# The skip term of a Mamba layer moved from a VectorE operation into a PSUM accumulation on TensorE

## The reference

```
x, z = split(xn @ in_proj_w.T);  x = silu(conv4(x))          # 256 channels each
s_t = s_{t-1} * exp(delta_t * A) + (delta_t * x_t) * B_t      # 16 states per channel
y_t = sum over the 16 states of s_t * C_t
y = y + x * Dskip
y = y * silu(z)
out = y @ out_proj_w.T
```

## Time and profile before

| | |
|---|---|
| median of 3 runs | 1236.87 us (1236.36 to 1238.31) |
| span of the profiled execution, first to last instruction | 1232.9 us |
| DVE busy | 1070.5 us (87%) |
| PE busy | 1022.4 us (83%) |
| POOL busy | 858.9 us (70%) |
| ACT busy | 734.7 us (60%) |
| mean granted TensorE clock | 0.901 |

### The profile page before, as it was taken

The page is one execution under the profiler, slowest core; times in us unless marked ns, Lnnn a source line. Parts: engine busy times, 40 slices in busy tenths (PEclk is TensorE's granted clock), DMA queues, the critical chain, the costliest instruction groups (busy, mean ns, idle before and its releaser), DMA issues.

```text
span 1232.9 us, 15308 instructions
## 1 busy us (share of the span) xinstructions
PE 1022.4 (83%) x3821; PEld 476.4 (39%) x3821; DVE 1070.5 (87%) x1331; ACT 734.7 (60%) x1117; POOL 858.9 (70%) x708
## 2 busy tenths in 40 slices
PE   0755858999999899999999997888888888888785
PEld 0522324444545454444445453333333333243322
DVE  7647968889898979899898989999898989999996
ACT  2564535767586776767685766556564756555421
POOL 2335788767676867677676769687777868686755
PEclk9988868999999999999999999788887979797765
DMA  6542325243432424342534423442434333343311
GB/s 160 157 94 68 91 79 130 57 99 69 107 80 64 103 62 111 77 94 51 119 68 98 89 57 80 86 86 48 87 71 90 81 73 68 82 85 80 72 36 34
DMA packets 81065, 103.01 MB, mean 84 GB/s; under 512 B 13280, under 2 KB 51072, under 8 KB 81024
## 3 DMA queue, kind: packets, MB, share of 16 engines
q1 hardware_dynamic: 76928, 94.18, 35.3%
q0 software_dynamic: 4096, 8.40, 2.3%
HBM read 18.66 MB, written 16.78 MB: 29 GB/s over the span
## 4 chain that ended last, share of the span: by engine, by line
PE 40%; DVE 24%; issue 22%; POOL 7%; ACT 3%; DVEq 1%; DMA 1%; SPq 1%; POOLq 0%; ACTq 0%
DVE u_sb L902 10%; DVE s_sb L972 8%; PE bank L1204 6%; PE bank L1171 5%; PE bank L1189 5%; PE bank L1127 4%; PE bank L1182 4%; PE bank L1114 3%; POOL expert_in L585 3%; PE bank L1135 2%; PE bank L1136 2%; PE bank L1137 2%; POOL s_sb L578 2%; PE bank L1147 2%; DVE g_sb L860 2%
## 5 line engine op out<-in xcount | busy, mean ns | idle before, releaser
L578 POOL TENSOR_TENSOR s_sb<-s_sb,c_of 128x512 f32<-128x512 f32 x480 | 628.5, 1315 | 273.2 <-DVE s_sb L972 265.1
L972 DVE TENSOR_TENSOR_SCAN s_sb<-bank,u_sb 128x512 f32<-128x512 f32 x512 | 620.4, 1212 | 0.0
L762 ACT ACTIVATE bank<-bank,a_neg 128x510 f32<-128x510 f32 x512 | 334.0, 659 | 255.9 <-PE bank L1189 246.4
L902 DVE TENSOR_TENSOR u_sb<-bank,b_of 128x512 f32<-128x512 f32 x512 | 346.2, 676 | 98.7 <-PE bank L1182 94.9
L1182 PE MATMUL bank<-dsp,sel_d 128*128 128x512 f32 x512 | 316.1, 617 | 39.8 <-DVE u_sb L902 20.4
L1189 PE MATMUL bank<-dsp,sel_d 128*128 128x512 f32 x512 | 244.5, 478 | 79.0 <-DVE s_sb L972 71.5
L1182 PEld LDWEIGHTS bank<-dsp,sel_d 128*128 128x128 f32 x512 | 104.6, 204 | 243.4 <-DVE u_sb L902 147.6
L1189 PEld LDWEIGHTS bank<-dsp,sel_d 128*128 128x128 f32 x512 | 106.5, 208 | 195.4 <-DVE s_sb L972 163.0
L1204 PE MATMUL bank<-s_sb,con 128*32 128x512 f32 x1024 | 161.2, 706 | 12.7 <-POOL s_sb L578 6.8
L1114 PE MATMUL bank<-xnT,wx 128*128 (+1 forms) x256 | 128.8, 597 | 0.0
L585 POOL DMA_INDIRECT expert_in<-xn,put_at x64 | 65.6, 1026 | 17.9 <-issue 17.8
(11 more groups left out here) (140 smaller groups left out, 1045.0 us busy)
## 6 DMA issues: line engine op xcount, KB each, us to landing
b_of<-bc SPq DMA_DIRECT2D x64, 256.0 KB
c_of<-bc SPq DMA_DIRECT2D x64, 256.0 KB
dsp<-hi SPq DMA_DIRECT2D x64, 256.0 KB
dsp<-dd SPq DMA_DIRECT2D x64, 256.0 KB
expert_in<-dd SPq DMA_DIRECT2D x8, 512.0 KB, 6.4
xn<-expert_in SPq DMA_DIRECT2D x8, 512.0 KB, 5.4
xn<-L_ffn_W SPq DMA_DIRECT2D x16, 256.0 KB, 4.6
expert_out<-xn SPq DMA_DIRECT2D x16, 256.0 KB, 2.4
```

The costliest lines, as they stand in the source:

```text
L578: pool.tensor_tensor(s_now, s_now, c_of[:, hf, hh, :], ALU.mult).then_inc(S["p_ready"], 1)
L762: act.activation(d, d, ACT.Exp, scale=a_neg[:, k:k + 1]).then_inc(S["decay_ready"], 1)
L902: dve.tensor_tensor(u_sb[:, w % U_RING, :], du_ps[w % 2][:, :], b_of[:, hf, head_of(w), :], ALU.mult).then_inc(S["u_ready"], 1)
L972: dve.tensor_tensor_scan(s_sb[:, w % S_RING, :], decay_of(w)[:, :], u_sb[:, w % U_RING, :], 0.0, ALU.mult, ALU.add).then_inc(S["scan_done" ...
```

## The change

A diagonal matrix skip_w with Dskip on its diagonal is made once for each half in the setup. In sum_quad, before the first sum of a half, PE multiplies x by it with start=True; the sums that follow all accumulate. `gate_half` is one product of the PSUM bank and silu(z). The semaphore y_read is gone: PE's first write to the bank in the next half waits for g_ready.

```diff
-GATE = (5, 6)
+GATE = 5
...
+        skip_w = sb("skip_w", [P, HALVES, P])
...
+            dve.wait_ge(S["w_loaded"], 16 * W_LOADS)
+            for hf in range(HALVES):
+                dve.tensor_scalar(skip_w[:, hf, :], ident, dsk[:, hf:hf + 1], None, ALU.mult
+                                  ).then_inc(S["skip_ready"], 1)
...
-            def gate_half(ch, hf, step):
-
-                if step == 0:
-                    dve.wait_ge(S["sum_done"], per_chunk(ch, SLOTS // QUADS, UNITS // QUADS * (hf + 1)))
-                    dve.scalar_tensor_tensor(g_sb[:, hf, :], xs_of(ch, hf), dsk[:, hf:hf + 1], y_ps[:, :],
-                                             ALU.mult, ALU.add).then_inc(S["y_read"], 1)
-                else:
-                    dve.wait_ge(S["y_read"], per_chunk(ch, 2, hf + 1))
-                    dve.tensor_tensor(g_sb[:, hf, :], g_sb[:, hf, :], zs_of(ch, hf), ALU.mult
-                                      ).then_inc(S["g_ready"], 1)
+            def gate_half(ch, hf):
+
+                dve.wait_ge(S["sum_done"], per_chunk(ch, SLOTS // QUADS, UNITS // QUADS * (hf + 1)))
+                dve.tensor_tensor(g_sb[:, hf, :], y_ps[:, :], zs_of(ch, hf), ALU.mult).then_inc(S["g_ready"], 1)
...
-                    wait(pe, "y_read", per_chunk(ch, 2, k * QUADS // UNITS))
+                    hf = k * QUADS // UNITS
+                    wait(pe, "g_ready", per_chunk(ch, 2, hf))
+                    pe.matmul(y_ps[:, :], skip_w[:, hf, :], xs_of(ch, hf), start=True, stop=False)
                 wait_products(pe, ch, QUADS * (k + 1))
                 for q in range(QUADS):
                     mm = pe.matmul(y_ps[q * 32:(q + 1) * 32, :], con[:, K_SUM + 32 * r:K_SUM + 32 * (r + 1)],
                                    s_sb[:, (QUADS * k + q) % S_RING, :],
-                                   start=(r == 0), stop=(r == UNITS // QUADS - 1))
+                                   start=False, stop=(r == UNITS // QUADS - 1))
...
+            pe.wait_ge(S["skip_ready"], HALVES)
```

More of the change, by code:

```diff
@@ L197, in bass_mamba_moe @@
             "scattered du_spread delta_spread u_ready decay_ready scan_done p_dve p_ready sum_done "
-            "y_read g_ready misc_pe misc_act misc_dve misc_bc b_loaded0 b_loaded1 c_loaded0 c_loaded1 sp_act sp_chain "
+            "skip_ready g_ready misc_pe misc_act misc_dve misc_bc b_loaded0 b_loaded1 c_loaded0 c_loaded1 sp_act sp_chain "
             "dx_ready dd_ready hi_ready lo_ready stacked ffn_loaded eo_free b1_ready take_ready back_loaded "
@@ L980, in body @@
                                           ).then_inc(S["p_dve"], 1)
[L982 to L986, removed]
+                    if w == GATE and ch[0] > 0:
+                        gate_half(before(ch), 1)
+                    if w == UNITS + GATE:
+                        gate_half(ch, 0)
                     if not low_by_pool(ch):
@@ L1015, in last @@
                 ins.then_inc(S["combine_last"], 1)
-                gate_half(end, 1, 0)
-                gate_half(end, 1, 1)
+                gate_half(end, 1)
                 dve.wait_ge(S["combine_last"], 1)
```

## The result

The changed kernel took 1245.36 us (median of 4 runs, 1245.09 to 1247.75), the kernel before 1236.76 in the same rounds (1236.36 to 1238.31). The ratio is 1.0074, with a 95% interval of 1.006 to 1.0089: slower by 8.6 us, where 4.9 us of gain were forecast, and outside the range given.

The account below looks back on a forecast made before the run. No engine bounds everywhere: DVE and PE alternate within a chunk. Gains of 1.1 (expert chunks), 0.6 (combine chunks) and 3.2 us (last chunk) sum to 4.9, giving 1232.0 us from 1236.9, range 1225.5 to 1239.0.

Parts of the forecast that it names:

- First gate: Expert chunk, first gate: L1200 delays spreads and B/C matmul, which starts 0.33 us late; less old slack, +0.2 us.
- old slack at L872: Expert chunk, end of the output projection: under 0.1 us to spare at L872 on DVE, taken off the 0.33 us delay.
- Second gate: Expert chunk, second gate: L1200 fills PE's pauses, second layer starts at 579.0 instead of 579.36, a gain of 0.35 us.
- rival 1: PE is the bound behind each gate: expert-chunk gates lose 0.35 us each, slow-clock gates 0.3, kernel 1241 us; chance 0.17.
- Combine chunks: Chunks 9 to 14: gain 0 at the first gate, 0.1 us a chunk taken overall, 0.6 us for six.
- quoted rule: VectorE with two SBUF inputs contends with GpSimd reading SBUF; the new gate frees POOL, but the sum stays the same.
- clock rival: L1200 fills PE's gaps in combine chunks, the clock rises, second gates gain 0.6 instead of 0.1: 1228 us; chance 0.13.
- 1.8 us for L1200 at half clock: Combine chunks, second gate: clock at 0.50, L1200 costs 1.8 us, u comes 0.2 to 0.3 late.
- gain of 0 around the first gate: Combine chunks, first gate: ACT is held by POOL's memset and DVE's next u waits for PE, so gain 0.
- DVE's saving: The one-product gate saves DVE 0.63 us a half, 20.2 us over 32 halves if DVE set the pace everywhere.
- Last chunk and tail: PE has room for L1200: first gate gains 1.4 us, second 1.0, tail's L860 0.8, together 3.2 us.

Follow-up runs that it names:

- e1: Changed kernel with the skip matmul on PE, but DVE keeping both gate steps (first with factor zero): 1242.6 us, ratio 1.0053 to the kernel before.
- e3: Changed kernel with skip matmuls moved in PE's order, half 0's behind the third sum (slot 14), half 1's behind slot 23's expert matmul: 1232.47 us, ratio 0.9977.
- e10: e6 with half 1's skip matmul ahead of slot 23's expert matmul instead of behind it: one run of 1239.38 us.
- e6: Changed kernel with half 0's skip matmul in slot 8, ahead of the B/C matmul, and half 1's in slot 23 behind the expert matmul: 1233.21 us, ratio 0.9996.
- e2: Changed kernel with the one-operation gate on DVE but no skip matmul, so x * Dskip is left out: 1236.76 us, ratio 1.0007.
- e7: e6 with the combine operations from slot 16 on: 1223.74 us, ratio 0.9922.
- e9: e6 with the combine operations of chunks 9 to 14 in slots 18 to 25: 1225.54 us, ratio 0.992.
- e11: e6 with both gate steps kept on DVE (first with factor zero): 1234.89 us, ratio 0.9998.
- e8: The kernel before with only the combine operations moved, from slot 16 on: 1242.12 us, ratio 1.007.
- e4: Changed kernel with the combine operations of chunks 9 to 14 in slots 16 to 23 instead of 14 to 21: 1229.28 us, ratio 0.9946.
- e5: e3 and e4 together, skip matmuls in slots 14 and 23 and combine operations from slot 16 on: 1225.05 us, ratio 0.9923.

## Why the prediction was wrong

Two steps failed in their reasoning: in the expert chunks the start of the second layer, put at 579.0 without its wait for ACT, and in the combine chunks the time of DVE's operations between the gates, taken as constant. A third had the right mechanism and a wrong size, the first gate of an expert chunk.

**First gate (forecast +0.2 us, measured +0.5).** The mechanism was the forecast one, the size was off. The working had the second spread at 2.92 behind the gate and the B/C matmul at 6.57; they stand at 3.10 and 6.74. L1200 with the change of weights took 1.05 from its start to the sum's, not 0.98, and it started 0.72 behind the gate, where the forecast had 0.71. The remaining 0.1 lies between the sum's start and the second spread (1.33 against 1.23). And of the old slack at L872, from which the forecast took its way down from 0.33 to 0.2, nothing was had: L871 is later by the whole 0.5. e1 (+0.55) and e3 (-0.06) show that it is L1200's place.

**Second gate (forecast -0.35, measured +0.23).** This step failed in its reasoning. "The second layer starts at 579.0" assumed that it follows the spreads of slot 24, which came at 4.60 behind the gate as worked out (4.58). It depends on ACT's relu of the expert matmul that L1200 pushed back. In the timeline of the kernel before, at the end of the stretch of the earlier trace rows:

```profile
577.04 1.02 PE L1164 MATMUL bank<-xn 128*128 128x512 f32 x2
...
578.21 0.68 ACT L737 ACTIVATE xn<-bank,b_now 128x512 f32<-128x512 f32 x1
...
579.36 1.95 PE L1171 MATMUL bank<-xn 128*128 128x128 f32 x16
```

The relu ends at 578.89, 1.85 us behind the expert matmul's start and inside the 0.63 us that PE waits for the scan up to 579.02, so no wait for ACT was to be seen. In the changed kernel the expert matmul stands 3.51 behind the gate, and with those 1.85 the relu can't be ready before 5.36 by this row; measured, L1168 starts at 5.31. The forecast spent a pause of PE without asking what else it covered. e10 against e6 shows the link, by 0.58 us. The two gates together cost 0.73 us a quiet expert chunk, about the 0.70 of rival 1, which had a chance of 0.17; but rival 1 put the second gate's loss on PE's time alone.

**Clock in expert chunks (not forecast).** In one of chunks 3 to 8 the clock fell, for 1.5 us. The change made the wait before the B/C matmul 1.91 us instead of 0.93; PE's part alone makes it 1.49 (e1) and DVE's part alone 1.53 (e2). In the kernel before a wait of 0.63 us for a scan stands shortly ahead of it, so PE's idle time grew by less than these numbers say. In the eight traces, those of before and of the change among them, in which this wait is 0.91 us or more, 12 of the 56 chunks 2 to 8 have a stretch at half clock, one to three in each trace. In e6, e7, e9 and e10, where it is 0.68 at most, and in e11, where PE doesn't wait there, none of 35 has one. So with the pause filled no such fall was seen.

But the length of the wait doesn't tell which chunk falls: 1.91 us gave one fall and 1.53 three, and e8, whose expert chunks are those of the kernel before, has one in chunk 8. The Trainium skill, TensorE: Matmul & The Clock Gate, section HAM oscillation, says that idle gaps bring the clock down; e6 agrees in this, as filling the gap left chunks 2 to 8 at 1.00, and the 44 chunks that kept full clock with the gap show that the gap alone doesn't decide.

**Combine chunks (forecast -0.1 each, measured +1.1 to +2.3 in chunks 10 to 14).** The forecast looked at the two gates only. From L872 in slot 11 to slot 18 DVE runs without a wait, and I took its operations there as constants. One of them is 1.6 us longer because of POOL's run.

Five chunks with 1.6 make 8.1 us, and the +8.05 measured equals it only because the other slots cancel over the five: some 13 us are gained, 6.0 of them in slots 6 and 22 and 6.8 in slot 27, and as much is lost, in slots 1, 7 to 11, 19, 23 and 31. Only the long operation is the same in each of the five; the step from +1.1 to +2.3 is that of slots 19 and 23. e1, whose slots 1, 27 and 31 show nearly the changed kernel's pattern, has none of the five long operations and stands at +0.35: beside it the changed kernel has lost 8.1 us more in slot 14, and what it lost more in slots 7 to 11, 19 and 23 (6.9) about returned what the gates gave (6.0).

The same operations moved by two slots change the span by -15.5 us in e4, and by +4.9 in e8, on the kernel before. e1 and e2 show that it is DVE's part of the change that brings the long operations, e11 that it isn't the saved operation by itself. What decides is one interval, from DVE's L872 to the start of POOL's run. The kernel before, the changed one and the six versions with the combine operations in slot 14 have 48 such chunks: in 37 the run begins 0.04 to 1.24 us behind L872, and each has a long operation, the longer the later the run; in 11 it begins 0.46 to 1.22 us ahead, and none has one. That a chunk without a long operation is shorter as a whole isn't shown: chunks 10 to 14 are at +1.99 in e3 with five that cost 11.3 us in slot 14, and at -2.31 in e7 with five, and e9 is no faster than e7.

The quoted rule of the Trainium skill (SBUF — State Buffer, Who interferes with whom) was drawn on for L864 and POOL, and dismissed as of no effect on the sum. The same rule names the pair that decided: a combine operation is a VectorE one with two SBUF inputs, and the traces agree with the rule there, 0.33 us with no product running and 1.96 beside POOL's run.

**The clock rival was half true.** The forecast's 1.8 us for L1200 at half clock was not met: in the chunk shown it took 1.06, slot 22 gained the whole 0.60 us, and slot 27 1.37 where the clock had been at half. The mean clock of the combine window rose from 0.85 to 0.92. The gain was spent in the same chunk: slot 1 lost 0.4 to 1.05 us, slots 7 and 8 to 11 0.3 and 0.45, slot 31 0.4, and in every other chunk slot 19 lost 1.1 and slot 23 0.7. The forecast's gain of 0 around the first gate was thus some 0.2 of loss.

**DVE's saving.** 20.2 us of DVE work in the quiet rows were worth 0.38 us an expert chunk with no L1200 at all (e2), 0.27 beside one well placed (e11 to e6). In such a chunk of e6 slots 6 and 22 are 0.60 us shorter each, and slots 9, 11 and 26, where DVE waits for PE, 0.30, 0.30 and 0.46 longer. That DVE waits for PE, on which the forecast was built, held.

**Last chunk and tail (forecast -3.2, measured -2.1).** The tail's gate went as forecast. The chunk lost 1.40 in slot 7 again, of 1.61 gained in slot 6, and the tail waited 2.82 us for gathered rows where it had waited 2.40, so part of DVE's gain only made that wait longer.

**Open.** Why the half-clock stretches of the combine chunks fall where they do, and with them the 0.4 to 1.1 us in slots 1 and 19, was seen and not tested. Nor is it settled why e3, e6 and e11, each with six long operations, stand in chunks 10 to 14 at +1.99, +6.16 and +4.35. The 11.6 us between the changed kernel and e4 in these chunks is four times what its long operations account for: five of some 1.9 us gave way to three of some 2.0.

## What to carry to other kernels

When work is moved to an in-order engine, follow every consumer behind it through the other engines, and ask of each pause that it fills what the pause was covering. When an engine gets faster, look for what it will now run beside: an operation of constant work isn't one of constant time, and a shift of half a microsecond against another engine's burst brought 1.6 us a chunk here, where the two removed operations had given 1.2. When such a meeting is removed, measure again: its time can come back at the next wait, as in e9. The change paid after the order around it was changed too: with the combine operations two slots later 0.9946 (0.9929 to 0.9963), and with the matmuls also out of the chains behind the gates 0.9923 (e5) and 0.9922 (0.9893 to 0.995, e7), instead of 1.0074.

## What the runs showed of the hardware

A combine operation of 128x128 with both large inputs in SBUF took 0.32 to 0.34 us in all 657 cases of the 13 traces in which no POOL product was running when it started, also in the 540 of them in which one began 0.15 us later. Where one product was already running and no other followed, it took 0.70 to 1.36, and beside a run of products without a gap 1.88 to 3.07. All 46 operations of over 1.5 us ended with the run: DVE's next operation starts 0.07 to 0.08 us behind the end of the run's last product. Such an operation was not slowed by a share: it stood for the rest of the run, while the u and scan operations, with an input in PSUM, passed at their usual 0.68 and 1.21 us in the same run. The products beside it kept their pace (7.46 us for six, 1.24 each).

The other way round it is the DVE operation already running that counts: the products that began during the L864 of the kernel before, with both inputs in SBUF, took 1.64 us (median of 92 in the traces), and those that began during the new gate, with one input in PSUM, 1.29 (64). The 1.64 of the earlier trace rows and the 1.63 in the lines of e8 are of the first kind.

Mean granted clock and time of a kernel don't go together by themselves: the changed kernel had 0.923 to 0.926 in its four executions and was slower, and of the kernel before an execution of 1230.06 us had 0.919 and one of 1230.52 us had 0.902.
